# The turns of the next block's features behind the gate and up products in a spline feed-forward

## The reference

```python
gate_w = spline_reconstruct(gate_cp, INTER, HIDDEN)      # 1024 x 256 from 2033 control points
up_w = spline_reconstruct(up_cp, INTER, HIDDEN)
down_w = spline_reconstruct(down_cp, HIDDEN, INTER)
gate = jnp.einsum('bsh,ih->bsi', hidden_states, gate_w)
up = jnp.einsum('bsh,ih->bsi', hidden_states, up_w)
inter = jax.nn.silu(gate) * up
return jnp.einsum('bsi,hi->bsh', inter, down_w)
```

## Time and profile before

| | |
|---|---|
| median of 3 runs | 920.44 us (915.58 to 921.44) |
| the profiled execution | 921.88 us, its span 920.1 us |
| PE busy | 835.1 us, 91% |
| DVE busy | 645.0 us, 70% |
| ACT busy | 542.2 us, 59% |
| POOL busy | 324.6 us, 35% |
| granted PE clock, mean | 0.963 |

### The profile page before, as it was taken

One profiled execution on the slowest core, in us unless ns is written; L12 is line 12 of the kernel. 1 busy time (PEld: TensorE's weight loads), 2 busy tenths in 40 slices (PEclk: granted clock), 3 DMA queues, 4 the chain that ended last, 5 costly groups with the idle time before them and its releaser, 6 DMA issues.

```text
span 920.1 us, 21455 instructions
## 1 busy us (share of the span) xinstructions
PE 835.1 (91%) x7348; PEld 711.8 (77%) x7348; DVE 645.0 (70%) x1287; ACT 542.2 (59%) x1062; POOL 324.6 (35%) x386
## 2 busy tenths in 40 slices
PE   4599899999999997889999998999998499999997
PEld 3467676777777775688888897899997388888887
DVE  7566777777778775467777766788888167777765
ACT  2146445555554544466666676688886266666664
POOL 2932222222322324333333321167666533333320
PEclk9779999999999999799999999999999599999999
DMA  5955666755765652000000000000000000000001
GB/s 170 121 80 83 129 98 95 98 83 86 99 93 89 91 80 49 17 1 1 1 0 0 1 1 1 1 0 1 0 1 1 1 1 24 25 23 23 24 25 46
DMA packets 33751, 40.54 MB, mean 44 GB/s; under 512 B 4319, under 2 KB 25216, under 8 KB 33648
## 3 DMA queue, kind: packets, MB, share of 16 engines
q1 hardware_dynamic: 33690, 39.74, 26.2%
HBM read 8.79 MB, written 5.24 MB: 15 GB/s over the span
## 4 chain that ended last, share of the span: by engine, by line
PE 51%; DVE 16%; ACT 13%; issue 10%; POOL 4%; SPq 2%; DMA 2%; ACTq 1%; DVEq 1%; POOLq 0%
PE bank L396 6%; DVE inter L1731 6%; PE bank L397 5%; PE bank L398 5%; PE pair_a L805 5%; ACT stk L1355 4%; ACT gact L1360 4%; PE bank L819 4%; PE bank L1005 3%; PE pair_b L774 3%; DVE in_lo L1736 2%; PE pair_b L1129 2%; DVE st L1705 2%; PE bank L1015 2%; PE bank L1129 2%
## 5 line engine op out<-in xcount | busy, mean ns | idle before, releaser
L1231 ACT ACTIVATE prob<-pair_a 128x768 f32<-128x768 f32 x128 | 103.7, 810 | 97.9 <-PE pair_a L805 96.8
L573 POOL TENSOR_SCALAR_AFFINE_SELECT prob<-prob 128x512 f32<-128x512 f32 x128 | 82.3, 643 | 214.5 <-ACT prob L1231 214.5
L396 PE MATMUL bank<-wd_hi,in_hi 128*128 128x256 f32 x512 | 147.3, 288 | 7.6 <-DVE X L1742 6.8
L1736 DVE TENSOR_TENSOR in_lo<-inter,in_hi 128x512 fp32r<-128x512 f32 x128 | 97.8, 764 | 79.8 <-ACT in_hi L1368 79.2
L398 PE MATMUL bank<-wd_hi,in_lo 128*128 128x256 f32 x512 | 142.9, 279 | 0.0
L397 PE MATMUL bank<-wd_lo,in_hi 128*128 128x256 f32 x512 | 142.7, 279 | 0.0
L1368 ACT ACTIVATE in_hi<-inter 128x512 fp32r<-128x512 f32 x128 | 80.9, 632 | 94.8 <-DVE inter L1731 94.8
L1578 DVE TENSOR_REDUCE mx<-pair_b 128x6 f32<-128x768 f32 x124 | 118.1, 953 | 17.4 <-PE pair_b L786 15.6
L1731 DVE TENSOR_TENSOR inter<-gact,pair_b 128x512 f32<-128x512 f32 x128 | 87.6, 684 | 50.2 <-ACT gact L1360 44.0
L396 PEld LDWEIGHTS bank<-wd_hi,in_hi 128*128 128x128 f32 x512 | 96.7, 189 | 15.6 <-issue 6.0
L397 PEld LDWEIGHTS bank<-wd_lo,in_hi 128*128 128x128 f32 x512 | 97.2, 190 | 3.6
(11 more groups left out here) (222 smaller groups left out, 2107.8 us busy)
## 6 DMA issues: line engine op xcount, KB each, us to landing
stack<-stage SPq DMA_DIRECT2D x192, 128.0 KB, 4.7
result<-X SPq DMA_DIRECT2D x8, 512.0 KB, 2.9
X<-in_attn_a_x SPq DMA_DIRECT2D x14, 256.0 KB, 5.0
stack<-mrow SPq DMA_DIRECT2D x128, 4.0 KB
wdx<-spline SPq DMA_DIRECT2D x1, 1024.0 KB
wd_lo<-wdx SPq DMA_DIRECT2D x16, 64.0 KB
spline<-factor_basis SPq DMA_DIRECT2D x1, 1008.0 KB, 6.9
X<-in_attn_a_x SPq DMA_DIRECT2D x1, 512.0 KB, 7.7
```

The source lines that it names most:

```text
L396: pe.matmul(dst, l_hi, r_hi, start=first, stop=False)
L573: pool.affine_select(out=diag, in_=diag, compare_op=ALU.is_ge, fill=0.0, base=0, pattern=[[0, 2], [0, 2], [1, P]], channel_multiplier=-1). ...
L1231: act.activation(prob[:, p % 4], pair_a[:, :, P:4 * P], ACT.Exp, scale=DK ** -0.5).then_inc(a_e, 1)
L1736: dve.tensor_tensor(in_lo[:, m % LAG, :], inter[:, m % 2, :], in_hi[:, m % LAG, :].bitcast(F32), ALU.subtract).then_inc(f_.il, 1)
```

## The change

In a step the turn of the next block is no longer issued ahead of the gate and up products but right behind them. The waits go with their instructions. PE's program alone changes; that of ACT, DVE, POOL and SP is the same word for word.

```diff
                 def period(g, u, prev=True, nxt=True, nxt2=True):
                     for m in range(MT):
-                        if m < MT - 1:
-                            turn_rows(g, u, m + 1)
-                        elif nxt:
-                            turn_rows(g + 1, 1 - u, 0)
                         pe.wait_ge(f_.st, upto(f_.st, base + g, m + 1))
                         pe.wait_ge(f_.si, upto(f_.si, base + g, m - 1))
                         pe.matmul(pair_a[:, m % 2, :], cst[:, 0, m, :], stk[:, m % 2, :], start=True,
                                   stop=True).then_inc(f_.gp, 1)
                         pe.wait_ge(f_.up, upto(f_.up, base + g, m - 1))
                         pe.matmul(pair_b[:, m % 2, :], cst[:, 1, m, :], stk[:, m % 2, :], start=True,
                                   stop=True).then_inc(f_.upp, 1)
+                        if m < MT - 1:
+                            turn_rows(g, u, m + 1)
+                        elif nxt:
+                            turn_rows(g + 1, 1 - u, 0)
                         if m in (2, 3) and nxt:
```

## The result

| | before | changed |
|---|---|---|
| median | 918.01 us of 4 runs (915.10 to 921.44) | 929.97 us of 4 runs (929.32 to 934.63) |
| the profiled execution | 921.88 us | 929.32 us |
| its span, mean granted PE clock | 920.1 us, 0.963 | 927.6 us, 0.959 |

The ratio is 1.0140, with an interval of 1.0085 to 1.0195. Timed again against more runs of the kernel before (16, median 919.47 us), the changed kernel gave 929.11 us and 1.0102 [1.0084, 1.0120]. So it is about 1% slower, as forecast: 929.7 us was stated, and the range was 923.0 to 934.0. That the median lies within 0.3 us of the forecast is luck in part. The forecast stood on a median of 920.44 us for the kernel before, which is 918.01 with one more run, and the loss is 9.6 us in the larger timing and 12.0 in the smaller, where 9.3 was worked out.

The account below looks back on a forecast made before the run. The prediction took a 22.72 us group cycle to be the bound, mostly ScalarE's and VectorE's chain, with PE's short part. Terms 6.72 + 0.34 + 0.98 + 1.22 = 9.3 us on 920.44 gave 929.7 us, range 923.0 to 934.0.

Parts of the forecast that it names:

- Step m = 5: In 14 groups, stk(6) and silu(5) behind it start 0.48 us later, as the turn follows both products; 6.7 us.
- Other steps of a full group: The turn comes 0.48 us later but is hidden while ScalarE is busy with the high part; no cost.
- Last group of the second feed-forward: At m = 3, stk(4) starts at 902.53 instead of 902.19, delaying the kernel's end once by 0.34 us.
- The two starts: At PE's low clock, turns behind products delay stk: 0.98 us in the first feed-forward, 1.22 in the second.
- Sum: Whole kernel: 6.72 + 0.34 + 0.98 + 1.22 = 9.3 us more, giving 929.7 us, 1.0% slower.
- Absorbed: Groups' 0.48 us goes into a wait not hanging on silu; only 2.5 us remain, 922.9 us; chance 0.15.
- The clock falls: Longer PE waits lower its clock in full groups: 25 us more, 955 us; three such groups 935; chance 0.08.
- Faster: silu gets its gate product 0.36 us sooner after each of 24 waits: 8.6 us less, 911.8 us; chance 0.03.
- The rule weighed ahead of the result: Keep the Matmul engine busy (first half); where it waits, speed up engines on the critical path (second half); no size.

Follow-up runs that it names:

- the first experiment: The changed kernel, but in step m = 5 of each group the turn stands ahead of the two products again; 921.98 us, ratio 1.0042.
- the one with the largest delay: The kernel before, but in step m = 5 alone the turn stands behind both products and half the down product; 939.89 us, ratio 1.0219.

## Why the forecast held, and where it was off

- **Step m = 5: 0.48 us, 14 times.** Right. stk(6) starts 4.36 us behind the moment products now and 3.87 before (545.40 against 541.04, 541.48 against 537.61), 0.49 later, and 0.46 to 0.49 reach the length of a group. 12 intervals between moment products give 5.7 us, where the sum has 5.8 for 12. One step alone makes it, and one step alone takes it away. The path behind silu(5) was misread in its first round: the chain passes from the product by up to DVE's statistics (L1705) and on to the next product, and not over the high part, stk and silu(6). The delay passes on all the same, since the statistics wait behind that product.
- **Other steps of a full group: nothing.** Right for the changed kernel. For m = 6 the reason was half of it: besides the late m = 5, DVE's statistics cover it, but not in the last full group, as the first experiment showed.
- **Last group of the second feed-forward: 0.34 us.** Right in size and place. stk(4) comes at 909.11 with 0.22 of idle, 2.73 us behind the one before it, where it was 2.42. From the last moment products to the end of the span the kernel takes 37.65 us instead of 36.81, 0.84, where the 14th delay and this one make 0.82. In the first feed-forward the same place was taken as covered, and it is: from the last moments to the first matmul of L1094 in the next stage it takes 46.57 instead of 46.02 us, and 0.49 of these 0.55 are the delay of its seventh m = 5.
- **The two starts: 0.98 and 1.22 us.** Here the term was mis-sized. stk(1) and stk(2) of the second one came at +0.95 and +1.17, as worked out. The step that failed is the silent one behind them, that the sum stops at "stk(2) comes at 738.91": from the third round on the ring of ScalarE and VectorE was to set the pace again. At the low clock the ring through the turn is the longer one, and the low clock lasts longer. Together the two cost 1.9 us in the second start, where 1.22 was worked out, and 1.1 us in the first, where 0.98 was, as means over eight profiles. The starts hold 3.1 us, not 2.2. How much of the 1.9 us is the clock was not measured apart.
- **Sum.** 5.7 in the intervals, 0.84 and 0.55 in the ends, 3.1 in the starts make about 10.2 us, where 9.3 was forecast. The two timings against the kernel before give 1.0140 and 1.0102 of 918 to 919 us, 9.4 to 12.9 us. The two profiled executions themselves differ by 7.44 us only: the attention ended 1.2 us earlier in the one after, and its GLA stage had its low clock later (the window from 710 to 715 us has a mean clock of 0.74 before and 1.00 after), while nothing of its program changed. A difference of two profiled executions would have been a poor measure of this change; its distances inside the feed-forward were a good one.
- **Rivals.** *Absorbed* would have left the groups at 22.7 us; they grew. (Its 922.9 us lay just outside the range, and not mostly inside as the prediction says.) *The clock falls* needed granted clocks under 1.00 in full groups; there are none, not even with the turn behind half of the down product. Nor did PE wait longer in one piece: its longest idle in a full group is 0.70 us after the change (884.40) and was 0.74 before (877.81). The fall of the clock behind the longest wait in the last group of the first feed-forward, from which this rival had its price, is no fixed companion of such a wait. Among the eight profiles with silu behind stk that wait is 1.83 to 2.28 us, and the clock fell behind it in four (both kernels of this comparison among them) and not in the other four. The end of that feed-forward took 46.02 us with the fall (before) and 44.45 without it (the kernel with three turns behind at the start, whose last group is the same), so a fall costs 1.6 us, where 1.8 was worked out. The Trainium skill, "TensorE: Matmul & The Clock Gate", section "Part 4: PE-mode transpose", has it that transposes don't count as activity; the turn of stk and that of xr next to one another, which now stand in steps 2 and 3 of each full group, did not lower the clock here. *Faster* had the right mechanism for another kernel: it decides where silu waits for the gate product, and when ScalarE's order is turned round it does, and then the change brings 0.9%.

The rule weighed ahead of the result, in "Perfetto Trace Analysis", section "Optimization Strategies" of the Trainium skill, had two halves. The runs side with the second: the change gave PE its products first and lost 1%, while one line moved in the program of ScalarE, on the path, gained 1.3%. PE's busy share is 91% before, 91% after the change, and 91% with both edits at 898.5 us, so this share tells none of the three apart.

## What to carry to other kernels

Which of two pieces of work to issue first on PE, here the turn or the products, was decided by which consumer stands first in the program of the in-order engine that waits, and not by which piece is the nearer to the result. Read the idle before both consumers: the one with idle before it (stk, 0.30 us) wants its input first, and the one without (silu, 0.0 in 128) gets nothing from an early one; then ask whether the consumers' order is right, which here was worth 1.3%, and 2.1% together with the change. A step that looks free because another step pays for it can turn costly when that other is mended.

## What the runs showed of the hardware

- A product of 512 columns directly behind four transposes takes 0.32 us until the next one starts (495.95 to 496.27 in the earlier trace rows), and behind a down product 0.24 (498.07 to 498.31). The change doesn't save these 0.08 us, it moves them: the first down matmul behind the turn now takes 0.20 us until the next one (498.91 to 499.11), where the usual one takes 0.12.
- At the low clock a short idle in each round and a late rise of the clock go together: 10.6 to 13.5 us after the first turn with 0.69 us of idle in each round of 2.76, and 5.5 to 9.9 us with the turn ahead. With the turn ahead and silu first, where PE idles 0.69 to 0.75 us in each round, it took 10.5 us. I had taken the price of the start as the same work at half speed, and not that the low clock could last longer with such an order. That the one causes the other is not shown.
- At full clock, idle pieces of up to 0.74 us on PE in a full group (before the down product, at 877.81 in the kernel before and at 894.16 in the one with the largest delay) left the granted clock at 1.00 throughout the groups. After the wait of 1.83 to 2.28 us in the last group of the first feed-forward it fell to 0.50 in four profiles of eight.
